# The conditioning by row, moved from a setup of its own to beside the first attention blocks

## The chip, the cores and the metric

One core of a Trainium2 chip. The metric is device time of one launch in microseconds (us); shorter is better. The median of three runs of the kernel before is 1063.24 us (1062.80 to 1065.88). The profiled execution took 1059.56 us.

## The reference

Two transformer layers on x of 8 batches x 512 rows x 128 channels, float32. Each layer has an attention and a feed-forward part, each modulated by six vectors per batch, which come from a condition c (8 x 128):

```python
mod = silu(c) @ wmod                      # 8 x 768: six vectors of 128 channels for each batch
sa, ca, ga, sb, cb, gb = split(mod, 6)    # names of the kernel: shift, scale and gate, twice
x = x + gate(ga) * attention(layernorm(x) * (1 + ca) + sa)
x = x + gate(gb) * ffn(layernorm(x) * (1 + cb) + sb)
```

Layer 0 is a plain one-headed softmax attention over 512 rows, then a gated feed-forward part whose operands are quantised in blocks of 16 (FP4 grid). Layer 1 is an attention of 16 heads with a decayed bias by position, then a feed-forward part with ternary weights.

## The kernel before, in words

Five engines each run one list of instructions, written out by Python generators that are stepped in a fixed interleaving; semaphores tie the lists together. `Chip.gate` (L70 on) is a barrier of all five engines, followed by the clearing of semaphores and by a second barrier.

**Setup** (`prepare`, from L149). SP's queue issues the loads in order: the conditions and `wmod` (L181, L182), seven side loads (L184 to L187), the eight batches of X (L189), the weights of both attentions (L1097, L1099). ACT makes Sigmoid and Ln of the decay logits (L1388 to L1392), Silu of the condition (L199), copies of the modulation (`mod`, L203), the powers of the decay (L1403 to L1405). PE multiplies by `wmod` in two forms: with batches as rows (L230), and with channels as rows (`by_channel`, L237). DVE makes decay tables (L1439 to L1451) and from `mod` the gates by row; from L267 on it adds the projected value bias, then splits the table `full` into three bfloat16 `parts` (L274 to L281). PE spreads each batch's row over all 128 partitions by a matmul with a 0/1 matrix, in two halves per batch (L245), and ACT (L208) and DVE (L285, L286) copy the halves to `rows`. DVE then copies the `chan` values (L289). POOL makes masks and constants up to L1425. A gate closes the setup.

**Layer 0** (`layer0`, from L888) runs attention and feed-forward as two threads. `attention0` has 48 blocks u, batch g = u / 4 and quarter a = u mod 4; 32 of them have attention work. In a block: DVE's row maximum of the scores (L481), ACT's Exp (L520), PE's transposes (L441), the next block's scores (L434), ACT's copy (L527). Beside these run the projections of the next batch: DVE's statistics (L356 to L367), POOL's power and shift (L375, L377), ACT's normalised rows (L387), PE's transposes (L339), ACT's modulated `hT` with `chan` (L391), and q, k, v (PE L343, L346, L350; ACT L396, L401, L406). Batch 0's projection stands ahead of block 0. DVE's `complete_dve` (L1455 to L1459) is in block 2. The residual uses `ga0` of `rows` (DVE L495, in u = 6 for batch 0), and POOL adds the bias row `bg0` (L561).

In each block a function `go` is called for four or five slots (five if u is even). Slot f, counted over all blocks, steps the feed-forward thread, whose parts start at constants: the weights' quantisation at `WEIGHTS` = 5 (DVE in `quantise_dve`, L576 to L602, nine steps for each of three weights, 11 slots apart; POOL L611; PE L801; ACT L809), the rows' norm at 33, the first hidden part at 40, the halves at 60. The feed-forward thread uses PSUM banks 0 to 3, the attention banks 4 to 7. Slots from 159 on also begin layer 1's operands. A gate closes layer 0 (L947 on), and it clears 27 semaphores.

**Layer 1** is the rest of the program: attention, then feed-forward.

Of the kernel before, what the change touches and what calls it, by code (L numbers as in the profile page):

```python
# [148 lines left out]
def prepare(c, t, sh, ahead):  # L149


    pe, dve, act, pool, sp, bank = c.pe, c.dve, c.act, c.pool, c.sp, c.bank
    own = ExitStack()
    with own:
        s_x, s_cond, s_side = c.signals("0", "x cond side", own)
        s_clear, s_fill, s_pick, s_made, s_silu, s_mod, s_rows, s_bvo, s_chan = c.signals("0", "clear fill pick made silu mod rows bvo chan", own)
        s_copied, s_step, s_parts = c.signals("0", "copied step parts", own)
        s_spread, s_kept_act, s_kept_dve = c.signals("0", "spread kept_act kept_dve", own)
# [16 lines left out]
        part = lambda n: full[:, order.index(n) * D:(order.index(n) + 1) * D]  # L175
        gates_ = [("ga0", mod[0][:, 0:D]), ("ga1", mod[1][:, 0:D]), ("gb0", mod[0][:, 3 * D:4 * D]), ("gb1", mod[1][:, 3 * D:4 * D])]
        by_channel = ((0, "sa0", 0, 0.0), (0, "ca0", 1, 1.0), (1, "sa1", 0, 0.0), (1, "ca1", 1, 1.0), (1, "sb1", 3, 0.0), (1, "cb1", 4, 1.0))

        def on_sp():
            for l in range(2):  # L180
                sp.dma_start(cT[l], t[f"cT{l}"]).then_inc(s_cond, 16)  # L181
                sp.dma_start(wmod[l], t[f"wmod{l}"]).then_inc(s_cond, 16)  # L182
            for l in range(2):
                sp.dma_start(bout[l], t[f"bout{l}"].partition_broadcast(W3)).then_inc(s_side, 16)  # L184
                sp.dma_start(bv[l], t[f"bv{l}"]).then_inc(s_side, 16)
                sp.dma_start(wo[l], t[f"wo{l}"]).then_inc(s_side, 16)
            sp.dma_start(w3s, t["w3s"].partition_broadcast(W3)).then_inc(s_side, 16)  # L187
            for b in range(B):
                sp.dma_start(tiles(sh.x(b)), t["x"][b].rearrange("(t p) c -> p t c", p=P)).then_inc(s_x, 16)  # L189
# [20 lines left out]
        def on_pool():  # L210
            for l in range(2):
                g = pool.memset(cs[l], 0.0)
            g.then_inc(s_clear, 1)
            for x, value in ((pick, 0.0), (sh.ident, 0.0), (sh.identh, 0.0), (sh.maskh, 0.0), (sh.neghalf, -0.5)):
                g = pool.memset(x, value)
            g.then_inc(s_fill, 1)
            pool.wait_ge(s_fill, 1)
            for k in range(G3):
                pool.affine_select(out=pick, in_=pick, compare_op=ALU.not_equal, fill=1.0, base=-32 * k, pattern=[[-1, B]], channel_multiplier=1).then_inc(s_pick, 1)
                pool.wait_ge(s_pick, k + 1)  # L220
            for i in (sh.ident, sh.identh):
                pool.affine_select(out=i, in_=i, compare_op=ALU.not_equal, fill=1.0, base=0, pattern=[[-1, P]], channel_multiplier=1)
            pool.affine_select(out=sh.maskh, in_=sh.maskh, compare_op=ALU.is_ge, fill=-1e30, base=0, pattern=[[-1, P]], channel_multiplier=1).then_inc(s_made, 1)
            pool.wait_ge(s_made, 1)
            ahead.constants_pool()

        def on_pe():
            pe.wait_ge(s_silu, 1)
            for l in range(2):
                m = pe.matmul(bank[1 + l][0:W3, :], cs[l], wmod[l][:, 2 * D:6 * D], start=True, stop=True)  # L230
            m.then_inc(s_mod, 1)
            pe.wait_ge(s_side, 7 * 16)
            for l in range(2):
                m = pe.matmul(bank[3][0:W3, l * D:(l + 1) * D], bv[l].to_broadcast([P, W3]), wo[l], start=True, stop=True)
            m.then_inc(s_bvo, 1)
            for i, (l, n, j, one) in enumerate(by_channel):
                m = pe.matmul(bank[0][:, i * B:(i + 1) * B], wmod[l][:, j * D:(j + 1) * D], cs[l][:, 0:B], start=True, stop=True)  # L237
            m.then_inc(s_chan, 1)
            pe.wait_ge(s_parts, 1)
            pe.wait_ge(s_pick, G3)  # L240
            for b in range(B):
                for half in range(2):
                    if b >= 2:
                        pe.wait_ge((s_kept_act, s_kept_dve)[half], b - 1)
                    pe.matmul(bank[4 + (2 * b + half) % 4], pick[:, b:b + 1].to_broadcast([W3, P]), parts[:, half * 512:(half + 1) * 512], start=True, stop=True).then_inc(s_spread, 1)  # L245

        def on_dve():
            ahead.tables_dve()
            dve.wait_ge(s_copied, 1)
            for k, (n, g) in enumerate(gates_):  # L250
                dve.tensor_scalar(tmp[k], g, 0.0, 0.5, ALU.is_ge, ALU.subtract)
                v = dve.scalar_tensor_tensor(tmp[4 + k], g, -1.0, g, ALU.mult, ALU.max)
            v.then_inc(s_step, 1)
            dve.tensor_copy(part("sb0"), mod[0][:, D:2 * D])
            dve.tensor_scalar(part("cb0"), mod[0][:, 2 * D:3 * D], 1.0, None, ALU.add)
            dve.wait_ge(s_step, 1)
            for k in range(4):
                v = dve.scalar_tensor_tensor(tmp[4 + k], tmp[4 + k], 0.25, tmp[k], ALU.max, ALU.mult)
            v.then_inc(s_step, 1)
            dve.wait_ge(s_step, 2)  # L260
            for k, (n, g) in enumerate(gates_):
                v = dve.tensor_scalar(part(n), tmp[4 + k], 2.0, None, ALU.mult)
            v.then_inc(s_step, 1)
            dve.wait_ge(s_bvo, 1)
            dve.wait_ge(s_side, 7 * 16)
            for l in range(2):
                v = dve.tensor_tensor(bvo[l], bank[3][0:W3, l * D:(l + 1) * D], bout[l], ALU.add)  # L267
            v.then_inc(s_step, 1)
            dve.wait_ge(s_step, 4)
            for l in range(2):  # L270
                dve.tensor_tensor(part(f"bg{l}"), part(f"ga{l}"), bvo[l], ALU.mult)
            dve.tensor_tensor(part("gb1"), part("gb1"), w3s, ALU.mult).then_inc(s_step, 1)
            dve.wait_ge(s_step, 5)
            dve.tensor_copy(parts, full).then_inc(s_step, 1)  # L274
            dve.wait_ge(s_step, 6)
            dve.tensor_tensor(left, full, parts, ALU.subtract).then_inc(s_step, 1)
            dve.wait_ge(s_step, 7)
            dve.tensor_copy(mid, left).then_inc(s_step, 1)
            dve.wait_ge(s_step, 8)
            dve.tensor_copy(parts[32:64, :], mid[32:64, :])  # L280
            dve.tensor_tensor(parts[64:W3, :], left[64:W3, :], mid[64:W3, :], ALU.subtract).then_inc(s_parts, 1)  # L281
            for b in range(B):
                dve.wait_ge(s_spread, 2 * b + 2)
                k = bank[4 + (2 * b + 1) % 4]
                dve.tensor_copy(sh.rows[1][:, b * D:(b + 1) * D], k[:, 0:D])  # L285
                dve.tensor_copy(sh.rows[2][:, b * 3 * D:(b + 1) * 3 * D], k[:, D:4 * D]).then_inc(s_kept_dve, 1)  # L286
            dve.wait_ge(s_chan, 1)
            for i, (l, n, j, one) in enumerate(by_channel):
                dve.tensor_scalar(sh.chan[n], bank[0][:, i * B:(i + 1) * B], one, None, ALU.add)  # L289

        on_sp()
        on_act()
        on_pool()
        on_pe()
# [1913 lines left out]
```

## Time and profile before

| | |
|---|---|
| median of three runs | 1063.24 us |
| profiled execution | 1059.56 us |
| its span, first to last instruction | 1058.3 us |
| busy PE, DVE, ACT, POOL | 869.2, 750.4, 659.3, 401.9 us |
| scores of block 0 end, gate of layer 0 | at 48.45 us, at about 342.7 us |

Times in the trace count from the first instruction. A row of the timeline has start, duration, engine, line, operation, and in brackets how long the engine was idle before it and what released it. A "q" behind an engine's name is its instruction queue (SPq issues DMAs). PEclk is the granted TensorE clock as a share of 2.4 GHz.

### The profile page before, as it was taken

Reading aid. Unit: us, or ns where it says so; the run is one execution under the profiler, and the core shown is the slowest. Engines: PE = TensorE matmul, PEld = TensorE weight load, DVE = VectorE, ACT = ScalarE, POOL = GpSimd, SP = SyncE. Lnnn points to the kernel's source line nnn. Section 1 sums busy time; section 2 is a strip of 40 time slices with the busy share of each in tenths; the row PEclk is TensorE's granted clock in tenths of the full one; section 3 lists DMA queues with packets and bytes.
Section 4 is the critical chain, followed back from the end, with each engine's and each line's share of the span. In section 5 each row is a group of like instructions: output and inputs, shape, how many; then the busy total and the mean of one; then the engine's idle time right before and its main releaser. Section 6 shows DMA issues by size and latency. Waiting matters only on the chain.

```text
span 1058.3 us, 25490 instructions
## 1 busy us (share of the span) xinstructions
PE 869.2 (82%) x9999; PEld 526.8 (50%) x9999; DVE 750.4 (71%) x1784; ACT 659.3 (62%) x1154; POOL 401.9 (38%) x664
## 2 busy tenths in 40 slices
PE   3577888877556689898989989899988868898987
PEld 1244455544335356565656656566655543444434
DVE  7366788888755778778687776868878647666653
ACT  4366878874522376756657566566666747776865
POOL 3024444444666547355354635437232210101000
PEclk7599999998967599999999999999999989999999
DMA  5000000000116235342523436154353000000000
GB/s 146 9 13 0 1 1 1 1 1 1 51 52 175 55 86 142 87 129 65 146 71 97 121 76 166 43 133 105 97 149 94 3 2 1 20 2 20 1 22 20
DMA packets 70698, 63.60 MB, mean 60 GB/s; under 512 B 30600, under 2 KB 62824, under 8 KB 70576
## 3 DMA queue, kind: packets, MB, share of 16 engines
q1 hardware_dynamic: 70064, 61.90, 22.1%
q8 instruction: 83, 1.36, 0.6%
q14 instruction: 39, 0.32, 0.1%
q10 hardware_dynamic: 512, 0.02, 0.0%
HBM read 34.02 MB, written 27.36 MB: 58 GB/s over the span
## 4 chain that ended last, share of the span: by engine, by line
PE 44%; DVE 11%; issue 6%; ACT 5%; POOL 2%; DVEq 0%; POOLq 0%; ACTq 0%
PE bank L2008 12%; PE bank L1589 7%; PE bank L1564 3%; PE bank L1537 3%; PE bank L1529 3%; PE bank L1545 3%; PE bank L1526 2%; PE bank L1519 2%; DVE bank L1672 1%; ACT 4g L2066 1%; PE bank L1555 1%; DVE 4f L2102 1%; PE bank L1597 1%; PE bank L1552 1%; DVE roots L1238 1%
## 5 line engine op out<-in xcount | busy, mean ns | idle before, releaser
L1750 ACT ACTIVATE ET<-bank 64x512 f32<-64x512 f32 x128 | 75.5, 590 | 101.4 <-PE bank L1555 100.5
L2089 DVE TENSOR_TENSOR act<-4f,act 128x512 f16<-128x512 f32 x96 | 66.4, 692 | 57.3 <-ACT act L2056 57.1
L1745 ACT ACTIVATE ET<-bank 128x768 f32<-128x768 f32 x128 | 103.2, 806 | 2.4
L1672 DVE TENSOR_TENSOR bank<-bank,W 128x256 f32<-128x256 f32 x128 | 54.7, 427 | 50.9 <-PE bank L1519 50.9
L1677 DVE TENSOR_TENSOR bank<-bank,WT 128x256 f32<-128x256 f32 x128 | 55.2, 431 | 49.9 <-PE bank L1545 49.9
L1682 DVE TENSOR_REDUCE mo<-bank 128x4 f32<-128x512 f32 x128 | 87.8, 686 | 2.7 <-PE bank L1529 2.5
L1589 PE MATMUL bank<-ET,vv 128*32 128x128 f32 (+2 forms) x1792 | 89.1, 323 | 0.8 <-DVE O L1707 0.8
L2056 ACT ACTIVATE act<-4f 128x512 f16<-128x512 f32 x96 | 60.4, 630 | 28.3 <-DVE 4f L2102 26.2
L1690 DVE TENSOR_REDUCE mo<-bank 128x3 f32<-128x384 f32 x128 | 70.0, 547 | 0.0
L1691 DVE TENSOR_REDUCE mo<-bank 128x3 f32<-128x384 f32 x128 | 69.9, 546 | 0.0
L1529 PE MATMUL bank<-maskq,identh 128*64 128x512 bf16 x256 | 62.7, 396 | 0.0
L2008 PE MATMUL bank<-act,std 128*128 128x512 f16 x256 | 58.1, 389 | 0.0
L2008 PE MATMUL bank<-act,cp 128*128 128x512 f16 x256 | 56.6, 379 | 0.0
L1526 PE MATMUL bank<-ring 128*64 128x128 f16 x256 | 28.1, 236 | 34.4 <-DVE bank L1672 34.4
L1589 PEld LDWEIGHTS bank<-ET,vv 128*32 128x32 f32 x1792 | 43.6, 109 | 23.8 <-issue 22.2
L1751 ACT ACTIVATE ET<-bank 64x256 f32<-64x256 f32 x128 | 48.6, 379 | 1.5
L2077 ACT ACTIVATE 4f<-bank,roots 128x512 f32<-128x512 f32 x64 | 43.3, 676 | 7.0 <-PE bank L2008 6.9
L1555 PE MATMUL bank<-maskk,identh 128*64 128x256 bf16 x256 | 47.3, 274 | 0.0
L1343 POOL TENSOR_TENSOR M<-cp 128x192 f32<-128x192 f32 (+2 forms) x48 | 23.4, 487 | 56.0 <-ACT cp L1294 54.9
L2126 POOL TENSOR_TENSOR X<-X,4Y 128x512 f32<-128x512 f32 x8 | 10.1, 1265 | 90.0 <-DVE 4Y L2115 90.0
L139 POOL TENSOR_TENSOR rstd<-ve,neghalf 128x4 f32<-128x4 f32 x8 | 9.3, 1164 | 91.9 <-DVE ve L121 91.9
L2008 PEld LDWEIGHTS bank<-act,std 128*128 128x128 f16 x256 | 25.7, 101 | 31.3 <-issue 3.6
(377 smaller groups left out, 2539.5 us busy)
## 6 DMA issues: line engine op xcount, KB each, us to landing
ring<-scr_q SPq DMA_DIRECT2D x16, 324.0 KB
QO<-scr_q SPq DMA_DIRECT2D x16, 324.0 KB
ring<-scr_a SPq DMA_DIRECT2D x16, 252.0 KB
KA<-scr_a SPq DMA_DIRECT2D x16, 252.0 KB
ring<-scr_k SPq DMA_DIRECT2D x16, 168.0 KB
KB<-scr_k SPq DMA_DIRECT2D x16, 168.0 KB
scr_a<-dk SPq DMA_DIRECT2D x8, 288.0 KB, 2.6
X<-in_x SPq DMA_DIRECT2D x8, 256.0 KB, 5.1
```

Of the source, the lines that this page charges most:

```text
L1529: m = pe.matmul(tiles(psD[z, :]), sh.identh[:, z], over(maskq, NT), start=False, stop=True, skip_group_check=True)
L1555: m = pe.matmul(half(psDT[z, :], 0), sh.identh[:, z], over(maskk, NT), start=False, stop=True, skip_group_check=True)
L1589: m = pe.matmul(psO[r:r + 32, c0:c1], vv[b % NV][:, v0:v0 + 32], ET[n % NE][:, e0:e0 + c1 - c0], start=c0 == 0, stop=k == NT - 1, skip_gro ...
L1672: dve.tensor_tensor(half(psD, 1), half(psD, 1), over(W[:, h * HB:(h + 1) * HB], NT), ALU.mult).then_inc(s_wq, 1)
L1682: dve.tensor_reduce(tiles(mo[g % 2][:, x * NT * NT:(x + 1) * NT * NT])[:, :, NT - 1], tiles(psD), AX.X, ALU.max).then_inc(s_ra, 1)
L1690: dve.tensor_reduce(to[:, 12:15], tiles(psX[:, 0:3 * P], 3), AX.X, ALU.max).then_inc(s_rb, 1)
L1691: dve.tensor_reduce(to[:, 6:11:2], tiles(psX[:, 512:512 + 3 * P], 3), AX.X, ALU.max).then_inc(s_rc, 1)
L1745: act.activation(ET[n % NE][:, T:SEG * P], psXT[:, 0:NP * P], ACT.Exp).then_inc(s_expo, 1)
L1750: act.activation(to[0:HB, :], psDT[0:HB, :], ACT.Exp)
L2008: m = pe.matmul(to, l, r, start=n == 0, stop=n == len(todo) - 1)
L2056: act.activation(act_[s][layer % 2][0][:, o * T:(o + 1) * T], f32_[f % 3], ACT.Copy).then_inc(s_hi, 1)
L2089: dve.tensor_tensor(lo, f32_[f % 3], hi, ALU.subtract).then_inc(s_lo, 1)
```

## The change

`prepare` has no barrier and no clearing of its own any more. It is called by `ffn0`, which passes it the first attention's thread. Its work is cut in two. The first part, ahead of block 0, keeps the loads, Silu, both products with `wmod` (`by_channel` first now), the gates by row and the decay tables, and takes in batch 0's statistics, normalised rows and `hT`. The second part (`rest`) is stepped once per slot f from slot 0 on: the value bias product, the making of `parts`, the spreading of the eight batches and the copies to `rows`. Waits that the barrier used to cover are written out.

```diff
 def on_sp():
     for l in range(2):  # cT and wmod, as before
+    sp.dma_start(tiles(sh.x(0)), ...).then_inc(s_x, 16)
+    ahead.load_first_sp()                 # wqkv0, wo0, bqk0
     ... seven side loads
-    for b in range(B): x -> s_x
-    ahead.load_sp()
-    sp.wait_ge(s_x, 16 * B)
+    for b in range(1, B): x -> s_rest
+    ahead.load_sp()
 def on_act():
-    ahead.decay_act()
+    ahead.load_act()
     ... wait s_cond, s_clear; Silu into cs
+    ahead.decay_act()                     # Sigmoid alone
+    first.begin_act(5)                    # batch 0's normalised rows
+    act.wait_ge(s_chans, 1)
+    first.begin_act(3)                    # batch 0's hT
     ... wait s_mod; copies to mod
-    ahead.powers_act()
-    for b in range(B): ... rows[0]
+    ahead.log_act()                       # Ln
 def on_pe():
     pe.wait_ge(s_silu, 1)
+    ... by_channel matmuls, s_chan
     ... mod matmuls, s_mod
-    ... bias matmuls; by_channel; spread
+    pe.wait_ge(s_made, 1)
 def on_dve():
+    dve.wait_ge(s_x, 16)
+    first.begin_dve()                     # batch 0's statistics
+    ahead.clamp_dve()
+    dve.wait_ge(s_chan, 1)
+    ... chan copies, s_chans
+    first.scale_dve()
     ahead.tables_dve()
     ... gates by row, as before
-    ... bias rows, parts, copies to rows, chan
+    ahead.exponents_dve()
+def rest_pe():
+    pe.wait_ge(s_side, 7 * 16)
+    ... bias matmuls, s_bvo
+    yield from blank(PARTS + 2)           # PARTS = 3
+    pe.wait_ge(s_parts, 1)
+    pe.wait_ge(s_pick, G3)
+    for b in range(B):
+        for half in range(2):
+            if b >= 2:
+                pe.wait_ge((s_rows, s_kept_dve)[half], b - 1)
+            pe.matmul(bank[(2 * b + half) % 4], ...).then_inc(s_spread, 1)
+        yield
+def rest_dve():
+    yield
+    ... bvo, bg, gb1
+    yield
+    ... parts, left
+    yield
+    ... mid, parts
+    yield from blank(PARTS)
+    for b in range(B):
+        dve.wait_ge(s_spread, 2 * b + 2)
+        ... two copies to rows[1], rows[2]
+        yield
+def rest_act():
+    yield from ahead.powers_act()         # three steps
+    yield from blank(PARTS)
+    for b in range(B):
+        act.wait_ge(s_spread, 2 * b + 1)
+        ... copy to rows[0]
+        yield
 # project_dve(b)
+        if b == 1:
+            dve.wait_ge(s_rest, 16 * (B - 1))
 # residual(g) on DVE
+            else:
+                dve.wait_ge(s_rows, B)
 # on_pool of attention0: bias row bg0
-            if a == 1 and g < B:
-                pool.wait_ge(s_xh, g + 1)
-                ... x(g) += bg0(g)
+            if a == 0 and 1 <= g <= B:
+                pool.wait_ge(s_xh, g)
+                if g == 1:
+                    pool.wait_ge(s_rows, B)
+                ... x(g - 1) += bg0(g - 1)
 # ffn0
-    WEIGHTS, ROWS, HIDDEN, MAIN, CYCLE = 5, 33, 40, 60, 18
+    WEIGHTS, ROWS, HIDDEN, MAIN, CYCLE = 17, 33, 40, 60, 18
 # layer0
     def go():
+        step(rest)
         step(thread)
         slot(next(f))
-    c.clear(first.signals)
+    c.clear(first.signals + [4 more] + rest.signals)   # 46 semaphores
 # complete_dve
+        dve.wait_ge(s_pow, 1)
```

Buffers of the setup (`full`, `parts` and so on) share their place with later feed-forward buffers, and the weights' own buffers no longer share it.

## Rows read from the trace of the kernel before

**Rows 1.** The page's first line.

```profile
span 1058.3 us, 25490 instructions
```

**Rows 2.** Windows: start:end, length, busy by engine (count), granted clock, DMA.

```profile
0.00:48.45 48.45, 20.66 (x54) 8.65 (x54) 25.03 (x81) 19.50 (x36) 9.29 (x36) 0.70 0.30 80
48.45:63.25 14.80, 9.79 (x27) 4.40 (x26) 10.56 (x31) 7.71 (x16) 2.43 (x3) 0.73 0.13 37
63.25:92.05 28.80, 21.71 (x94) 12.27 (x95) 16.28 (x62) 17.67 (x39) 12.40 (x14) 1.00 0.00 1
```

**Rows 3.** Timeline of SP's queue, and the DMA view's row of X.

```profile
2.70 0.43 SPq L184 DMA_DIRECT2D bout<-in_bout  x1
...
6.01 6.05 SPq L189 DMA_DIRECT2D X<-in_x  x8
...
X<-in_x SPq DMA_DIRECT2D x8, 256.0 KB, 5.1
```

**Rows 4.** Timeline of the setup, 5 to 23 us.

```profile
5.47 1.28 ACT L1391 ACT_TABLE_LOAD   x1
...
7.57 1.89 POOL L1425 MEMSET vv<- 128x608 f32 x3
...
8.39 0.70 ACT L199 ACTIVATE cs<-cT 128x8 f32<-128x8 f32 x6
...
9.14 3.40 PE L230 MATMUL bank<-wmod,cs 128*96 128x512 f32 x4 [9.14 <-ACT cs L199]
...
12.58 1.08 ACT L203 ACTIVATE mod<-bank 96x512 f32<-96x512 f32 x2 [3.49 <-PE bank L230]
...
12.81 1.40 PE L237 MATMUL bank<-cs,wmod 128*128 128x8 f32 x12
...
17.51 0.48 DVE L267 TENSOR_TENSOR bvo<-bank,bout 96x128 f32<-96x128 f32 x2
...
23.16 6.57 PE L245 MATMUL bank<-parts,pick 96*128 96x512 bf16 x16 [8.94 <-DVE parts L281]
```

**Rows 5.** Groups of instructions, 9 to 31 us: count, busy us, mean ns.

```profile
L286 DVE COPY rows<-bank 128x384 f32<-128x384 f32 x8 | 4.4, 547 | 0.0
...
L285 DVE COPY rows<-bank 128x128 f32<-128x128 f32 x8 | 2.3, 290 | 1.7 <-PE bank L245 1.1
```

**Rows 6.** Timeline of batch 0's projection, behind the gate.

```profile
32.09 0.86 DVE L356 BATCH_NORM_STATS2 stats<-X 128x6 f32<-128x128 f32 x4
...
34.90 0.20 POOL L377 TENSOR_TENSOR 1shift<-1nmean,rstd 128x4 f32<-128x4 f32 x1
35.22 1.65 ACT L387 ACTIVATE ring<-X,1shift,rstd 128x128 f32<-128x128 f32 x4 [5.07 <-POOL 1shift L377]
...
37.01 1.08 PE L339 MATMUL bank<-ident,ring 128*128 128x128 f32 x4 [7.28 <-ACT ring L387]
38.13 0.78 ACT L391 ACTIVATE ring<-bank,sa,ca 128x512 f32<-128x512 f32 x1 [1.27 <-PE bank L339]
...
41.82 2.08 PE L346 MATMUL bank<-ring,roots 128*128 128x512 f32 x2 [0.78 <-ACT ring L396]
...
48.49 0.69 DVE L481 TENSOR_REDUCE nm<-bank 128x1 f32<-128x512 f32 x1 [14.86 <-PE bank L434]
```

**Rows 7.** Timeline of blocks 1 to 3 and 8, DVE and PE.

```profile
52.91 0.69 DVE L481 TENSOR_REDUCE nm<-bank 128x1 f32<-128x512 f32 x1 [1.09 <-PE bank L434]
...
57.66 0.69 DVE L481 TENSOR_REDUCE nm<-bank 128x1 f32<-128x512 f32 x1 [0.95 <-PE bank L434]
...
59.64 0.56 DVE L599 TENSOR_TENSOR qb_u<-qb_u,qb_w 128x384 f32<-128x384 f32 x1
...
60.87 1.02 PE L346 MATMUL bank<-ring,roots 128*128 128x512 f32 x2
...
...
91.45 0.69 DVE L576 TENSOR_REDUCE qa_amax<-hm 128x32 f32<-128x512 f32 x1 [6.38 <-POOL hm L711]
```

**Rows 8.** One line's instructions (clearing of semaphores, L81): min/median/max ns.

```profile
L81 DVEq EVENT_SEMAPHORE_RANGE_CLEAR  x15: 54/54/56, 31.3 to 343.3; - x15
```

More of the change, by code:

```diff
@@ L146, in blank, with prepare @@
         yield
-def prepare(c, t, sh, ahead):
+class Thread:
+    pass
+def prepare(c, t, sh, ahead, first):
     pe, dve, act, pool, sp, bank = c.pe, c.dve, c.act, c.pool, c.sp, c.bank
+    s_cond, s_side = c.signals("0", "cond side", ahead.layer0)
+    s_clear, s_fill, s_pick, s_made, s_silu, s_mod, s_bvo, s_chan = c.signals("0", "clear fill pick made silu mod bvo chan", ahead.layer0)
+    s_copied, s_step, s_parts = c.signals("0", "copied step parts", ahead.layer0)
+    s_spread, s_kept_dve = c.signals("0", "spread kept_dve", ahead.layer0)
+    s_x, s_rest, s_chans, s_rows = first.s_x, first.s_rest, first.s_chans, first.s_rows
+    G3, W3 = 3, 96
+    order = [n for g in GROUPS for n in g]
     own = ExitStack()
     with own:
[L155 to L158, printed above, removed]
         sb = lambda *a, **k: c.sb(*a, at=own, **k)
-        G3, W3 = 3, 96
-        order = [n for g in GROUPS for n in g]
         cT = [sb(f"cT{l}", B) for l in range(2)]
@@ L174, in prepare @@
         pick = sb("pick", B, dt=BF16, rows=W3)
[L175 to L189, printed above, removed]
-            ahead.load_sp()
-            sp.wait_ge(s_x, 16 * B)
@@ L210, in on_pool @@
[L210 to L294, printed above, removed]
-        on_dve()
-        c.gate()
-        c.clear([s_x, s_cond, s_side, s_clear, s_fill, s_pick, s_made, s_silu, s_mod, s_rows, s_bvo, s_chan, s_copied, s_step, s_parts, s_spread, s_kept_act, s_kept_dve])
-        c.gate()
-class Thread:
-    pass
+    part = lambda n: full[:, order.index(n) * D:(order.index(n) + 1) * D]
+    gates_ = [("ga0", mod[0][:, 0:D]), ("ga1", mod[1][:, 0:D]), ("gb0", mod[0][:, 3 * D:4 * D]), ("gb1", mod[1][:, 3 * D:4 * D])]
@@ new lines, in prepare, with on_sp @@
+    by_channel = ((0, "sa0", 0, 0.0), (0, "ca0", 1, 1.0), (1, "sa1", 0, 0.0), (1, "ca1", 1, 1.0), (1, "sb1", 3, 0.0), (1, "cb1", 4, 1.0))
+    PARTS = 3
+    spread = lambda b, half: bank[(2 * b + half) % 4]
+    def on_sp():
+        for l in range(2):
+            sp.dma_start(cT[l], t[f"cT{l}"]).then_inc(s_cond, 16)
+            sp.dma_start(wmod[l], t[f"wmod{l}"]).then_inc(s_cond, 16)
+        sp.dma_start(tiles(sh.x(0)), t["x"][0].rearrange("(t p) c -> p t c", p=P)).then_inc(s_x, 16)
+        ahead.load_first_sp()
+        for l in range(2):
+            sp.dma_start(bout[l], t[f"bout{l}"].partition_broadcast(W3)).then_inc(s_side, 16)
+            sp.dma_start(bv[l], t[f"bv{l}"]).then_inc(s_side, 16)
+            sp.dma_start(wo[l], t[f"wo{l}"]).then_inc(s_side, 16)
+        sp.dma_start(w3s, t["w3s"].partition_broadcast(W3)).then_inc(s_side, 16)
+        for b in range(1, B):
+            sp.dma_start(tiles(sh.x(b)), t["x"][b].rearrange("(t p) c -> p t c", p=P)).then_inc(s_rest, 16)
+        ahead.load_sp()
@@ new lines, in on_act @@
+    def on_act():
+        ahead.load_act()
+        act.wait_ge(s_cond, 64)
+        act.wait_ge(s_clear, 1)
+        for l in range(2):
+            for g in range(G3):
+                a = act.activation(cs[l][:, 32 * g:32 * g + B], cT[l], ACT.Silu)
+        a.then_inc(s_silu, 1)
+        ahead.decay_act()
+        first.begin_act(5)
+        act.wait_ge(s_chans, 1)
+        first.begin_act(3)
+        act.wait_ge(s_mod, 1)
+        for l in range(2):
+            a = act.activation(mod[l], bank[1 + l][0:W3, :], ACT.Copy)
+        a.then_inc(s_copied, 1)
+        ahead.log_act()
@@ new lines, in on_pe, with on_dve @@
+    def on_pe():
+        pe.wait_ge(s_silu, 1)
+        for i, (l, n, j, one) in enumerate(by_channel):
+            m = pe.matmul(bank[0][:, i * B:(i + 1) * B], wmod[l][:, j * D:(j + 1) * D], cs[l][:, 0:B], start=True, stop=True)
+        m.then_inc(s_chan, 1)
+        for l in range(2):
+            m = pe.matmul(bank[1 + l][0:W3, :], cs[l], wmod[l][:, 2 * D:6 * D], start=True, stop=True)
+        m.then_inc(s_mod, 1)
+        pe.wait_ge(s_made, 1)
+    def on_dve():
+        dve.wait_ge(s_x, 16)
+        first.begin_dve()
+        ahead.clamp_dve()
+        dve.wait_ge(s_chan, 1)
+        for i, (l, n, j, one) in enumerate(by_channel):
+            v = dve.tensor_scalar(sh.chan[n], bank[0][:, i * B:(i + 1) * B], one, None, ALU.add)
+        v.then_inc(s_chans, 1)
+        first.scale_dve()
+        ahead.tables_dve()
+        dve.wait_ge(s_copied, 1)
+        for k, (n, g) in enumerate(gates_):
+            dve.tensor_scalar(tmp[k], g, 0.0, 0.5, ALU.is_ge, ALU.subtract)
+            v = dve.scalar_tensor_tensor(tmp[4 + k], g, -1.0, g, ALU.mult, ALU.max)
+        v.then_inc(s_step, 1)
+        dve.tensor_copy(part("sb0"), mod[0][:, D:2 * D])
+        dve.tensor_scalar(part("cb0"), mod[0][:, 2 * D:3 * D], 1.0, None, ALU.add)
+        dve.wait_ge(s_step, 1)
+        for k in range(4):
+            v = dve.scalar_tensor_tensor(tmp[4 + k], tmp[4 + k], 0.25, tmp[k], ALU.max, ALU.mult)
+        v.then_inc(s_step, 1)
+        dve.wait_ge(s_step, 2)
+        for k, (n, g) in enumerate(gates_):
+            v = dve.tensor_scalar(part(n), tmp[4 + k], 2.0, None, ALU.mult)
+        v.then_inc(s_step, 1)
+        ahead.exponents_dve()
@@ new lines, in rest_pe @@
+    def rest_pe():
+        pe.wait_ge(s_side, 7 * 16)
+        for l in range(2):
+            m = pe.matmul(bank[3][0:W3, l * D:(l + 1) * D], bv[l].to_broadcast([P, W3]), wo[l], start=True, stop=True)
+        m.then_inc(s_bvo, 1)
+        yield from blank(PARTS + 2)
[5 more added lines that the diff above has]
+                    pe.wait_ge((s_rows, s_kept_dve)[half], b - 1)
+                pe.matmul(spread(b, half), pick[:, b:b + 1].to_broadcast([W3, P]), parts[:, half * 512:(half + 1) * 512], start=True, stop=True).then_inc(s_spread, 1)
+            yield
@@ new lines, in rest_act @@
+    def rest_act():
[3 more added lines that the diff above has]
+            act.wait_ge(s_spread, 2 * b + 1)
+            act.activation(sh.rows[0][:, b * 4 * D:(b + 1) * 4 * D], spread(b, 0), ACT.Copy).then_inc(s_rows, 1)
+            yield
+    on_sp()
+    on_act()
+    on_pool()
+    on_pe()
+    on_dve()
+    rest = Thread()
+    rest.pe, rest.dve, rest.act, rest.signals = rest_pe, rest_dve, rest_act, [s_cond, s_side, s_clear, s_fill, s_pick, s_made, s_silu, s_mod, s_bvo, s_chan, s_copied, s_step, s_parts, s_spread, s_kept_dve]
@@ L305, in attention0 @@
+    return rest
 def attention0(c, t, sh, ahead):
@@ L318, in attention0 @@
     s_pv, s_out, s_rsum, s_proj, s_Y, s_add, s_bias = signals[20:27]
+    s_x, s_rest, s_chans, s_rows = c.signals("1", "x rest chans rows", ahead.layer0)
     wqkv, wo, bq, s_w = ahead.first_weights
@@ L626, in ffn0 @@
     s_hstep, s_hq, s_turn, s_kept, s_proj, s_Y, s_add = c.signals("2", "hstep hq turn kept proj Y add")
+    s_rows = first.s_add
+    names = ("wg", "wu", "wd")
+    wT = {n: sb(f"{n}T", FP) for n in names}
+    wr = {n: sb(f"{n}r", FP) for n in names}
+    room = lambda name, cols: [sb(f"{name}_{n}", cols // 16) for n in ("amax", "scale", "inv")] + [sb(f"{name}_{n}", cols) for n in ("u", "w")]
+    tmps_b = [room(f"qb{i}", 2 * FF) for i in range(2)]
+    rest = prepare(c, t, sh, ahead, first)
     xh, xq, Y, xqT = sb("2xh", T), sb("xq", T), sb("2Y", T), sb("xqT", T)
@@ L883, in ffn0 @@
     second = Thread()
+    second.rest = rest
     second.sp, second.pe, second.dve, second.act, second.pool, second.s_add = on_sp, on_pe, on_dve, on_act, on_pool, s_add
@@ L892, in layer0 @@
     first = attention0(c, t, sh, ahead)
-    second = ffn0(c, t, sh, ahead, first.s_add)
+    second = ffn0(c, t, sh, ahead, first)
+    rest = second.rest
     FREE = 159
@@ L943, in layer0 @@
     second.sp()
-    first.pe(beside(second.pe(), slot_pe))
-    first.act(beside(second.act(), slot_act))
-    first.dve(beside(second.dve(), slot_dve))
+    first.pe(beside(second.pe(), slot_pe, rest.pe()))
+    first.act(beside(second.act(), slot_act, rest.act()))
+    first.dve(beside(second.dve(), slot_dve, rest.dve()))
     first.pool(beside(second.pool(), slot_pool))
     c.gate()
-    c.clear(first.signals)
+    c.clear(first.signals + [first.s_x, first.s_rest, first.s_chans, first.s_rows] + rest.signals)
     c.gate()
```

97 lines of the change are left out of this document (64 added, 33 removed).

## The prediction

> **What bounds the kernel now.** I read the page for the span [rows 1], then windows of my own cut at the first score block, then the timeline of what stands ahead of it. The span is 1058.3 us. The profiled execution took 1059.56, 3.7 under the median of 1063.24; I work out a difference from the trace and take it off the median. About 0.3% (3.2 us) is what a measurement of this kernel can tell from no change.
>
> The first 48.45 us are poorly filled: PE works 20.7 of them, DVE 25.0, ACT 19.5 [rows 2]. What the reader is to see in the timeline is one long serial chain. The conditioning by row is DVE work until the spreading matmuls start at 23.16 [rows 4], and these with their copies go on until about 31. Only behind the gate, at 32.09, do batch 0's statistics start, and the first maximum of scores at 48.49 [rows 6]. None of the projection's inputs needs the rows: it needs X(0), `wqkv` and `chan`. From there on blocks follow each other as chains maximum, Exp, transposes, scores, and everything later moves with them. So the question is when the maximum of block 0 comes, and how much of that start the first blocks give back.
>
> **Start of block 0 after the change.** X(0) takes the place in SP's queue that the first side load has, 2.70, and lands 5.1 later [rows 3]: 7.8. Statistics to the variance take 1.5 (they start at 32.09; POOL's shift starts at 34.90, behind a power of about 1.1) [rows 6], so 9.3. POOL is in its memsets until 9.46 [rows 4], so its power and shift run from 9.5 to 10.8, and ACT's normalised rows (1.65) from 10.9 to 12.6 [rows 6].
>
> PE: Silu ran at 8.39, behind a table load of 1.28 [rows 4]. Now that load is the first thing on ACT and hides behind the DMA. I take the second `wmod` (issued about 2.2, with X's 5.1 to land) at 7.3, Silu done at 8.1. `by_channel` (1.40) ends at 9.5, the products for `mod` (3.40) at 12.9 [rows 4]. Transposes (1.08) end at 14.1, and `hT` (0.78) at 14.9, since `chan` is ready by 11. The q product takes 2.08 as the k product does [rows 6], to 17.0. ACT meanwhile copies `mod` (1.08, to 16.0), loads Ln's table (1.28) and makes two short Ln (about 0.3): 17.6 [rows 4]. So Ln, not PE, releases q's copy, at a price of 0.6. The copy (0.7) ends at 18.3. From the k product to the maximum it took 48.49 − 41.82 = 6.7 [rows 6]: block 0 starts at **25.0**, 23.5 us earlier.
>
> Is DVE there in time? Of its 25.0 us busy [rows 2] the part from 17.51 to 23.16, 5.6 us [rows 4], and the row copies, 4.4 + 2.3 = 6.7 [rows 5], leave. 12.7 stay. From 7.8 on they would be over at 20.5; the wait for `mod` at 16.0, once the tables are made, adds about 3: 23.5, just ahead of 25.0. DVE is the next stream to be late.
>
> The queues: SP issues X(0) past seven side loads, and the side loads and X(1) to X(7) wait behind the first weights. Eight X issues took 6.05 [rows 3], so the last X is issued by about 14 and lands by 19; batch 1's statistics ask for it at about 27. Side loads land by 13 and are asked for at 25. These edits cost nothing as long as the loads land within these 8 us; if not, DVE's queue stands still in block 0 by as much as is missing. POOL's bias row moves three blocks later and is still three quarters ahead of the residual's addition: nothing, and its new wait for the rows holds back POOL only if these come after block 4.
>
> **What the first blocks give back.** Slots 0 to 13 are blocks 0 to 2. They took 14.8 us [rows 2].
> - Block 0 (slots 0 to 4): DVE gets the 5.6 us of bias rows and parts in slots 1 to 3. It had 1.09 idle before the next maximum [rows 7]. Plus **4.5**. ACT's powers and the Exp table load (1.28, and about 1 us for each power) lie beside this, though the first delays the first Exp by about 0.7; DVE is longer, so it is not added.
> - Block 1 (slots 5 to 8): PE spreads batches 0 to 2 ahead of its transposes, a pair taking 6.57 / 8 = 0.8 at the lower clock [rows 4], and starts only when `parts` is there, as DVE's maximum does: 2.5 for PE. DVE's three pairs of copies take 2.5, against an idle 0.95 [rows 7]. DVE's count gives 1.6, PE's 2.5. I take **2.4**, since the transposes stand behind the matmuls.
> - Block 2 (slots 9 to 13): five more pairs of copies, 4.2, plus about 0.8 of waiting for matmuls that themselves wait for banks, less about 2.4 of weight quantisation that moves away. Plus **2.6**. `complete_dve` stays.
> Together 9.5. The bounds: nothing beyond DVE's bare excess gives 6; all 12.3 us of DVE work plus 0.8 with no cover gives 13. I keep 9.5: DVE was busy for 10.56 of these 14.8 us already [rows 2], so the cover is thin.
>
> **WEIGHTS from 5 to 17.** The weights' first two turns fall where the second and third fell. The third now runs in slots 39 to 47, beside the first hidden part. Seven of its nine DVE steps fall into blocks 9 and 10. One of the longest takes 0.56 [rows 7], so seven are at most 3.9; several work on 24 columns only, and I take 2.9; the first falls into the 6.38 us that DVE waits before 91.45 [rows 7]. Block 9 has idle time for half of it; the rest, and POOL's and PE's share, delay the first hidden part: **1.5**, between 0 and 6.
>
> **The end.** The gate of layer 0 clears 46 semaphores instead of 27 in three engines: 6.3 more at 54 ns [rows 8], with gaps **0.5**. The gate that is gone is in the 23.5.
>
> Sum: 23.5 − 9.5 − 1.5 − 0.5 = 12.0 faster: 1063.2 − 12.0 = **1051.3 us**.
>
> On table loads there is a rule. In the trace Ln's load takes 1.28, and the Ln starts at its end [rows 4]. The Trainium skill (ScalarE: Activation LUTs, "What ACT_TABLE_LOAD costs") gives the load the same time but adds a drain of about 1.38 to each switch. Two loads (Ln, Exp) could stand in the new chain, so by that rule the time would be some 2 to 3 us longer, 1054; the timeline before shows no such drain.
>
> **Rivals.**
> - *TensorE's clock is up sooner.* Before, the clock falls to 1.2 GHz in the idle stretches and averages 0.70 of full speed up to 48.45 [rows 2]; the k product takes 2.08 there and 1.02 once 2.4 GHz is granted [rows 6, 7]. Now PE's work lies closer together. Four such products in the chain at 1 us each, and 1 in block 1: 5 more, 1046. Against it: the projection's chain still has PE waiting for ACT between products. 0.15. The Trainium skill (TensorE: Matmul & The Clock Gate, "What's actually happening") lets the clock follow how busy PE was, which is the direction of this rival.
> - *The third weight delays the feed-forward's whole start.* Its 2.9 us on DVE, 0.8 on POOL, and PE's and ACT's short pieces all end up in front of the first hidden part: 6 instead of 1.5, 1056; for it, lists in fixed order; against it, idle time of DVE before 91.45. 0.15.
> - *The overlap is an illusion*: the moved work costs in the blocks what it cost before (13) and the weights 6: 1059 to 1062, no change. 0.07.
> - *Slower*: PE's waits for `parts` and for banks keep the clock at 1.2 GHz through blocks 3 to 8. These took 28.8 us with 21.7 us of PE at a clock of 1.00 [rows 2]; at half the clock that alone is 43.4, plus 14.6. With 2 more in blocks 1 and 2: 1068. It decides if projections in block 3 still take 2.08. Against it: PE is dense from block 1 on. 0.07.
> - That the change doesn't remove the gate can't be.
>
> **How the numbers follow.** The forecast of 1051 (1048 to 1055) has 0.56. The range takes in the clock's rival and the weights': 1045.5 to 1058. Faster by over 0.3% are forecast, clock and weights: 0.86. Within 0.3%: 0.07. Slower: 0.07.
>
> **What would show it.** In the changed profile: batch 0's statistics at 8, not 32; the first maximum at 25 (23 to 27); blocks 0 to 2 lasting 24 us; DVE idle-free through block 0; maximum of block 9 about 14 earlier than 92.05; layer 0's gate at 331. A first maximum after 30, or blocks 0 to 2 over 30, would make the forecast wrong.

## The result, and the profile of the changed kernel

The changed kernel takes 1045.45 us (median of 4 runs, 1043.87 to 1047.83) against 1064.03 for the kernel before (1062.80 to 1065.88, 4 runs): a ratio of 0.9824, interval 0.9804 to 0.9843, or 18.6 us. Forecast were 12.0, and 1045.5 as the lower end of the range. A second measurement in more rounds (below) gave a ratio of 0.9840 (0.9816 to 0.9864), 17.0 us. The kernel becomes faster, as forecast, but by about half as much again.

The windows of the changed kernel, cut at the same events as those of before: the maxima of blocks 0, 3, 9 and 31, and layer 1's first DVE work. Columns as in [rows 2].

```profile
0.00:26.19 26.19, 14.12 (x36) 7.90 (x37) 11.40 (x56) 11.47 (x24) 9.09 (x36) 0.87 0.54 147
26.19:47.81 21.62, 13.82 (x53) 6.92 (x52) 18.01 (x47) 14.76 (x29) 1.75 (x2) 0.84 0.09 25
47.81:74.43 26.62, 22.49 (x83) 12.10 (x82) 17.49 (x64) 16.07 (x37) 11.28 (x13) 0.87 0.00 1
74.43:215.78 141.35, 118.75 (x555) 73.09 (x553) 118.29 (x306) 115.96 (x202) 64.74 (x58) 1.00 0.00 1
215.78:326.28 110.50, 68.02 (x299) 47.14 (x300) 76.34 (x157) 42.52 (x79) 70.42 (x79) 0.80 0.24 68
326.28:1042.60 716.32, 630.19 (x8986) 382.14 (x8984) 505.35 (x1159) 456.74 (x786) 248.99 (x478) 0.97 0.27 72
```

Beside the same stretches of before, that gives a ledger (us; plus is time gained):

| stretch | before | after | gained | forecast |
|---|---|---|---|---|
| up to the first maximum | 48.49 | 26.19 | +22.3 | +23.5 |
| blocks 0 to 2 | 14.76 | 21.62 | −6.9 | −9.5 |
| blocks 3 to 8 | 28.80 | 26.62 | +2.2 | 0 |
| blocks 9 to 30 | 142.61 | 141.35 | +1.3 | −1.5 |
| block 31 to the end of layer 0 | 108.96 | 110.50 | −1.5 | −0.5 |
| layer 1 | 714.68 | 716.32 | −1.6 | 0 |
| sum | 1058.3 | 1042.6 | +15.7 | +12.0 |

The profiled executions are 1059.56 and 1043.87; the first lies 4.5 under its median and the second 1.6, which is the rest to 18.6. Two rows of the ledger say less than they seem to. Of the 1.3 in blocks 9 to 30, 1.7 are block 17, whose length changes by itself between executions (last section); without it the stretch is 0.4 longer. And the last two stretches, cut at DVE's last clearing of layer 0's semaphores, are 108.6 to 112.1 and 714.9 to 717.0 us long in seven of the traces (before, changed, experiments 1, 6, 7, 9 and 11), so their losses of 1.5 and 1.6 are within what two traces differ by.

The timeline of the changed setup, against [rows 4] and [rows 6]:

```profile
7.57 0.70 ACT L210 ACTIVATE cs<-cT 128x8 f32<-128x8 f32 x6 [3.58 <-DMA wmod<-in_wmod]
...
8.33 2.73 PE L242 MATMUL bank<-cs,wmod 128*128 128x8 f32 x12 [8.33 <-ACT cs L210]
8.41 0.87 DVE L393 BATCH_NORM_STATS2 stats<-X 128x6 f32<-128x128 f32 x4 [8.41 <-DMA X<-in_x]
...
10.91 3.71 PE L245 MATMUL bank<-wmod,cs 128*96 128x512 f32 x4
...
11.40 1.65 ACT L424 ACTIVATE ring<-X,1shift,rstd 128x128 f32<-128x128 f32 x4 [1.51 <-POOL 1shift L414]
...
14.41 1.06 PE L374 MATMUL bank<-ident,ring 128*128 128x128 f32 x4
...
16.40 1.12 PE L378 MATMUL bank<-ring,roots 128*128 128x512 f32 x2 [0.93 <-ACT ring L428]
17.33 1.28 ACT L1456 ACT_TABLE_LOAD   x1
...
18.62 0.21 ACT L1456 ACTIVATE lg<-lg 128x16 f32<-128x16 f32 x1
...
18.83 0.67 ACT L433 ACTIVATE ring<-bank,bq 128x512 f32<-128x512 f32 x1
...
26.19 0.69 DVE L518 TENSOR_REDUCE nm<-bank 128x1 f32<-128x512 f32 x1 [1.12 <-PE bank L471]
```

The reader is to see the forecast's chain, link by link: X(0) at 8.4 (forecast 7.8), the transposes held up by PE's own products with `wmod` (L245), and q's copy at 18.83 released by Ln, not by PE's product, which was over at 17.5. The last row shows DVE idle for 1.12 before the first maximum: DVE was in time, as forecast (25.1 against 26.2). Ln starts as its table's load of 1.28 ends; no drain stands between. The Trainium skill (ScalarE: Activation LUTs, "What ACT_TABLE_LOAD costs") adds one of about 1.38; by these rows the sum was right to leave it out.

The first blocks, against [rows 7]:

```profile
34.78 0.69 DVE L518 TENSOR_REDUCE nm<-bank 128x1 f32<-128x512 f32 x1
34.81 3.06 PE L288 MATMUL bank<-parts,pick 96*128 96x512 bf16 x6 [5.08 <-DVE parts L312]
...
40.56 0.69 DVE L518 TENSOR_REDUCE nm<-bank 128x1 f32<-128x512 f32 x1 [1.90 <-PE bank L471]
...
47.81 0.68 DVE L518 TENSOR_REDUCE nm<-bank 128x1 f32<-128x512 f32 x1
...
51.77 0.69 DVE L518 TENSOR_REDUCE nm<-bank 128x1 f32<-128x512 f32 x1 [2.82 <-PE bank L471]
```

Blocks 0 and 2 end without DVE idle: there DVE is the bound. Block 1 (5.8 us) waits for PE, whose spreading matmuls start only when `parts` is there. In block 3 DVE is idle for 2.82 again.

### The profile page after: what moved, and what is told of

Read it like the earlier page. It is cut to its first block, busy times and chain, and to the rows that moved or that the text cites. A ratio compares the mean times of both kernels' runs of the same rounds, so it can differ in the third digit from the quotient of the medians.

```text
span 1042.6 us, 25479 instructions
## 1 busy us (share of the span) xinstructions
PE 867.4 (83%) x9999; PEld 529.3 (51%) x9999; DVE 746.9 (72%) x1784; ACT 657.5 (63%) x1154; POOL 406.3 (39%) x664
## 4 chain that ended last, share of the span: by engine, by line
PE 45%; DVE 11%; issue 6%; ACT 5%; POOL 2%; DVEq 0%; POOLq 0%; ACTq 0%
PE bank L2081 12%; PE bank L1662 7%; PE bank L1637 3%; PE bank L1610 3%; PE bank L1602 3%; PE bank L1618 3%; PE bank L1599 2%; PE bank L1592 2%; DVE bank L1745 1%; ACT 4g L2139 1%; PE bank L1628 1%; DVE 4f L2175 1%; PE bank L1670 1%; PE bank L1625 1%; DVE roots L1299 1%
```

## The experiments

Times are compared by the ratio to the kernel before on the same chip; "over the changed kernel" is the difference of ratios to 0.9824, times 1064. By the second measurement of the changed kernel (0.9840) each such difference is 1.7 us smaller. Line numbers in rows are those of the changed kernel, plus up to five where an edit adds lines.

**1. The weights' later start alone, in the kernel before.**

```diff
-    WEIGHTS, ROWS, HIDDEN, MAIN, CYCLE = 5, 33, 40, 60, 18
+    WEIGHTS, ROWS, HIDDEN, MAIN, CYCLE = 17, 33, 40, 60, 18
```

> The kernel before with WEIGHTS = 17 alone; all is computed. Theory A (now mine): the later weights help, since the third weight's DVE, POOL, PE and ACT pieces no longer stand in front of batch 0's first hidden part; the stretch from block 3's to block 9's maximum falls from 28.8 us to about 26.6, and the time is 2 to 3 us under the kernel before. Theory B (the prediction's step): 1.5 us slower. Theory C (the 2.2 us seen in that stretch come from something else, such as the clock): no difference, within 1 us.

Measured: 1059.39, ratio 0.9940 (0.9920 to 0.9961): **6.0 us faster** than 1065.41 (4.2 to 8.5 by the interval), about twice what theory A said; theories B and C fall. So about a third of the whole gain needs no new order of the setup. Windows of this run from block 0's maximum to block 3's, block 9's and block 31's:

```profile
48.46:61.04 12.58, 8.96 (x25) 4.32 (x26) 7.19 (x21) 7.03 (x15) 2.43 (x3) 0.69 0.16 44
61.04:87.81 26.77, 22.40 (x89) 12.18 (x88) 17.09 (x64) 16.60 (x38) 11.29 (x13) 0.94 0.00 1
87.81:228.91 141.10, 118.76 (x555) 73.11 (x553) 119.53 (x306) 116.10 (x203) 62.56 (x58) 1.00 0.00 1
```

Against 14.76, 28.80 and 142.61 these are 2.2, 2.0 and 1.5 less. The first is DVE's: block 2 no longer holds the first weight's steps beside `complete_dve`. Of the second, 1.6 lie in block 8 and 0.7 in block 5. In block 8, before, ACT copied the third weight (from 85.59, after waiting for its transposition) ahead of the normed rows that the first hidden part is waiting for; in this run the norm goes first:

```profile
85.59 0.49 ACT L809 ACTIVATE wdT<-bank 128x384 f32<-128x384 f32 x1 [1.17 <-PE bank L801]
85.97 1.64 ACT L690 ACTIVATE 2xh<-X,shift,2rstd 128x128 f32<-128x128 f32 x4
```

```profile
81.70 1.64 ACT L690 ACTIVATE 2xh<-X,shift,2rstd 128x128 f32<-128x128 f32 x4
83.24 0.47 ACT L809 ACTIVATE wuT<-bank 128x384 f32<-128x384 f32 x1
87.21 0.69 DVE L576 TENSOR_REDUCE qa_amax<-hm 128x32 f32<-128x512 f32 x1 [3.62 <-POOL hm L711]
```

(the first of the kernel before, the second of this run; the changed kernel has the order of the second). Shift was ready at 84.16 before and at 81.51 here: 1.8 us of waiting became 0.2. DVE's first work on the hidden part, which stands ahead of block 9's maximum, comes 5.5 us behind the start of the norm in both (91.45 in [rows 7], 87.21 here), so block 9 gets the 1.6.

It is a matter of one slot. ACT copies the weights in slots 15, 26 and 37 before and in 27, 38 and 49 with `WEIGHTS` = 17; the norm is in slot 37, and where both share a slot the weight's copy comes first in ACT's list. The second weight now stands where the third stood, one slot later. `WEIGHTS` = 6, which would show this slot's worth by itself, was not run.

The third difference, 1.5, is block 17 (7.2 us before, 5.6 here), which is no effect of the edit (last section). So up to block 31 the trace shows 4.2 for the weights' move, the lower end of what the times show.

**2. The weights earlier in the changed kernel** (`WEIGHTS` = 9).

> The changed kernel with WEIGHTS = 9 in place of 17; all is computed. Theory A: the third weight is back in slots 31 to 39, in front of the first hidden part: about 2 us slower than the changed kernel, and the stretch from block 3's to block 9's maximum over 28 us. Theory B: 1.5 us faster than the changed kernel. Theory C: no difference.

Measured: 1050.79, ratio 0.9873 (0.9841 to 0.9906), 5.2 over the changed kernel. The direction is theory A's, the place is not: the stretch from block 3 to block 9 is 28.5, 1.9 more, but another 4.6 are lost in block 9 (8.0 us, in the changed kernel 3.4), of which block 10 gives 1.5 back. PE stands there:

```profile
76.87 0.84 POOL L663 TENSOR_TENSOR wdr<-qb_u,qb_scale 128x384 f32<-128x384 f32 x1
77.76 0.50 PEld L857 LDWEIGHTS bank<-ident,wdr 128*128 128x128 f32 x3 [7.03 <-POOL wdr L663]
77.76 0.90 PE L857 MATMUL bank<-ident,wdr 128*128 128x128 f32 x3 [6.20 <-POOL wdr L663]
```

DVE had finished this weight at 72.1. POOL took it up at 76.87, since its list has the next batch's power and shift, the first hidden part's modulation and a bias row before it; PE, in order, waited 6.20 with the attention's scores behind.

**3. The barrier back** (behind batch 0's `hT`).

```diff
+    first.begin_pe()      # batch 0's transposes, as before
+    first.begin_pool()    # batch 0's power and shift, as before
+    c.gate()
     second.sp()
```

> The changed kernel with one barrier of the five engines put back behind its setup, that is behind batch 0's hT and ahead of its q product. Theory A: the barrier costs what its last engine is late, and that is DVE with the exponents until 25.1 us, while q's product starts at 16.4: the first maximum comes at about 35.5 instead of 26.2, 9 us slower than the changed kernel. Rival: the barrier costs only its own drains, under 1 us, and the order of the work alone brings the gain.

Measured: 1055.87, ratio 0.9915 (0.9889 to 0.9941), 9.7 over the changed kernel; the first maximum is at 34.81, 8.6 later. DVE's last exponents and PE's wait for the barrier:

```profile
23.83 1.21 DVE L1527 TENSOR_TENSOR WT<-sq,bs 128x1024 f32<-128x1024 f32 x1
25.13 2.08 PE L378 MATMUL bank<-ring,roots 128*128 128x512 f32 x2 [9.68 <-DVEq L74]
```

PE waits 9.68 where it waited 0.93 without the barrier, and goes on 0.1 after DVE has ended (25.04). The rival falls: this barrier costs what its last engine is late.

**4. The second part in one piece** between block 0's scores and its maximum.

```diff
         scores(0)
+        step(beside.rest, 99)             # and so on DVE and ACT
...
         def go():
-            step(rest)
             step(thread)
```

> The changed kernel with the whole second part (value bias product, parts, spreading, copies to rows) run in one piece between block 0's scores and its maximum, not slot by slot. Theory A: idle time in blocks 0 to 2 covers nearly half of the moved work. In one piece it costs about 13 us ahead of the first maximum (39 instead of 26.2), blocks 0 to 2 fall from 21.6 to about 14.8, and the time is about 6 us over the changed kernel. Rival (the overlap is an illusion): as fast as the changed kernel, within 1 us.

Measured: 1055.13, ratio 0.9883 (0.9850 to 0.9916), 6.3 over the changed kernel. The first maximum is at 39.91 (13.7 later), and blocks 0 to 2 take 12.95, not 21.62. So the same work costs 13.7 in one piece and 8.7 slot by slot; blocks cover 5.0 of it. The rival falls.

```profile
39.91:52.86 12.95, 9.16 (x25) 4.22 (x26) 7.26 (x23) 6.92 (x15) 1.21 (x2) 0.74 0.16 42
```

This row also corrects the ledger: without the rest blocks 0 to 2 are 12.95 long, not 14.76, because the weights' move had emptied block 2 (12.58 in experiment 1).

**5. The bias row where it was** (block 4g + 1, waiting for all rows in block 1).

```diff
-            if a == 0 and 1 <= g <= B:
-                pool.wait_ge(s_xh, g)
-                if g == 1:
+            if a == 1 and g < B:
+                pool.wait_ge(s_xh, g + 1)
+                if g == 0:
```

> The changed kernel with POOL's bias row back where it was (block 4g + 1, so that for batch 0 POOL waits for all eight rows in block 1); all is computed. Theory A: nothing, within 1.5 us, for POOL has only batch 1's power before that and batch 2's power in block 4, long after the rows are there at about 47. Rival: the later place is needed, and POOL's standing wait holds up shift or weights: 2 us or more over the changed kernel.

Measured: 1047.25, ratio 0.9834 (0.9809 to 0.9859), 1.1 over the changed kernel, with intervals that overlap: the times tell no difference. The trace shows one of about that size. Block 2 is 8.3 us long instead of 7.25 (7.2 to 7.3 in experiments 3, 7, 8, 9 and 10). POOL's bias row of batch 0 now falls beside DVE's completion of the decay tables, and one small DVE instruction, 0.28 us in the changed kernel, lasts until the bias row has ended:

```profile
45.62 2.02 POOL L598 TENSOR_TENSOR X<-X,rows 128x512 f32<-128x512 f32 x1 [13.40 <-ACT rows L325]
46.43 1.29 DVE L1528 TENSOR_SCALAR Dq<-Dq,bsc 96x128 f32<-96x128 f32 x1
```

So the later place is worth about 1 us in block 2, though not for the reason that the rival names.

**6. The decay tables completed in block 3.**

```diff
-            if u == 2:
+            if u == 3:
                 ahead.complete_dve()
```

> The changed kernel with DVE's completion of the decay tables (2.7 us) in block 3 instead of block 2; all is computed. Theory A: block 2 (7.25 us) is bounded by DVE and block 3 has 2.8 us of DVE idle, so block 2 falls by about 2.4, block 3 stays, and the time is 2.4 us under the changed kernel. Rival: PE's spreading matmuls and their waits for banks bound block 2: no difference.

Measured: 1041.95, ratio 0.9791 (0.9769 to 0.9812), 3.5 under the changed kernel; the interval overlaps that of the first measurement (0.9804 to 0.9843) a little and that of the second (0.9816 to 0.9864) not. In the trace the maxima of blocks 2, 3 and 4 are at 38.75, 44.29 and 48.13: block 2 falls from 7.25 to 5.54, only 1.7, since then the last copy waits for PE (below); block 3 takes 3.8, not longer than the 4.0 of the changed kernel. The other 1.8 by which block 3 is earlier stood already at the first maximum (24.43), which this edit does not touch. So theory A holds with 1.7 for its 2.4.

```profile
43.62 0.29 DVE L316 COPY rows<-bank 128x128 f32<-128x128 f32 x1 [0.98 <-PE bank L288]
```

**7. PE kept busy ahead of Silu's products.**

```diff
 def on_pe():
+    pe.wait_ge(s_fill, 1)
+    for i in range(22):
+        pe.matmul(bank[6][:, 0:P], sh.neghalf, sh.neghalf, start=True, stop=True)
     pe.wait_ge(s_silu, 1)
```

> The changed kernel with 22 matmuls of constants (results overwritten unused) on PE from 1.7 to about 7.7 us, ahead of Silu's products; all is computed. Theory A (the prediction's clock rival): although the clock column says 1.00 up to 16 us, the products with wmod ran at the pace of 1.2 GHz (0.85 us for half of a 512-column product). With PE busy before, they halve: 6.1 us become about 3.2, the transposes come at 13.1 instead of 14.4, hT ends at 14.3, the first maximum comes 2 to 3 us earlier, and so does the end. Rival: the pace there is not the clock's; no difference.

Measured: 1042.84, ratio 0.9800 (0.9779 to 0.9822), 2.6 under the changed kernel, though the intervals overlap. The first maximum is at 23.62; in the traces whose setup is that of the changed kernel (its own and those of experiments 2, 5, 6, 8, 9 and 10) it lies between 24.43 and 26.21. So the edit gives 0.8 to 2.6 there.

```profile
1.74 7.33 PE L242 MATMUL bank<-neghalf 128*128 128x128 f32 x44 [1.74 <-POOL neghalf L227]
8.90 1.41 PE L245 MATMUL bank<-cs,wmod 128*128 128x8 f32 x12
10.16 1.94 PE L248 MATMUL bank<-wmod,cs 128*96 128x512 f32 x4
13.30 0.63 PE L377 MATMUL bank<-ident,ring 128*128 128x128 f32 x4 [1.21 <-ACT ring L427]
```

The products with `wmod` take 1.41 and 1.94 instead of 2.73 and 3.71: about half. The k product, too, takes 2.08 at 1.2 GHz and 1.02 at 2.4 [rows 6, 7]; so the changed kernel ran them at 1.2 GHz.

**8. The weights later still** (`WEIGHTS` = 20).

> The changed kernel with WEIGHTS = 20 in place of 17; all is computed. In slots 33 to 40 batch 0's rows are normed by a chain through DVE, POOL, ACT and POOL again; in the run with WEIGHTS = 9 PE stood 6.2 us for the third weight, which POOL had behind that chain. Theory A: what counts is that no weight's piece falls into that chain. With 20 the second weight's POOL piece is in slot 40 and PE's too, so it stands behind the chain as the third did with 9, and PE stands still: 4 to 6 us over the changed kernel. Theory B (the later the better, as DVE's load is what counts): 1 us faster than the changed kernel.

Measured: 1057.97, ratio 0.9942 (0.9921 to 0.9963), 12.6 over the changed kernel, twice what theory A said. "The later the better" falls. PE waits for the second weight, which POOL has behind the modulation, and for the third, which DVE works off beside the quantisation of the first rows (POOL itself waits 0.50 for it):

```profile
76.90 0.90 PE L857 MATMUL bank<-ident,wur 128*128 128x128 f32 x3 [6.21 <-POOL wur L663]
...
90.91 0.55 PE L857 MATMUL bank<-ident,wdr 128*128 128x128 f32 x3 [3.78 <-POOL wdr L663]
```

**9 to 11, on one chip: the changed kernel again, `WEIGHTS` = 14, and edits 6 and 7 together.**

> The changed kernel itself once more, on the same chip as the next two and in more rounds. All theories expect the ratio of the first measurement, 0.982 within 0.002. If it comes near 0.987, then the forecast of 12 us faster was right and the first measurement was off.

> The changed kernel with WEIGHTS = 14 in place of 17; all is computed. The weights' POOL and PE pieces fall on slots 23, 34 and 45; batch 0's chain of norms takes slots 33 to 40. Theory A (a piece costs only if PE meets it while POOL still has that chain ahead of it, as in slot 40): no difference to the changed kernel within 1.5 us, though DVE's load comes earlier. Theory B (the later the better): 1 to 3 us slower.

> The changed kernel with both edits that gained alone: the decay tables completed in block 3, and PE kept busy ahead of Silu's products; all is computed. If they act at different places (block 2, and the chain ahead of block 0) they add: 2.4 + 2 us under the changed kernel, ratio 0.978 to 0.976. Rival: DVE, which already ends the exponents just ahead of the first maximum, eats the second one: as fast as with the tables' move alone, 0.979.

Measured: 1048.21, ratio 0.9840 (0.9816 to 0.9864); 1050.85, ratio 0.9876 (0.9852 to 0.9900); 1040.79, ratio 0.9787 (0.9756 to 0.9818).

The first confirms 17 to 19 us, not 12. With 14 the kernel is 3.8 slower than with 17 on the same chip (the intervals overlap by 1.3 us), more than the 1.5 of theory A. It is nearest to theory B's 1 to 3, but experiment 8 speaks against "the later the better". Its trace names a place that I had not looked at: block 5 takes 6.2 us against 4.0, since the first weight's piece on PE (slot 23) meets POOL behind batch 2's power and shift and the bias row:

```profile
54.36 1.26 POOL L598 TENSOR_TENSOR X<-X,rows 128x512 f32<-128x512 f32 x1
...
55.59 0.83 POOL L663 TENSOR_TENSOR wgr<-qb_u,qb_scale 128x384 f32<-128x384 f32 x1
...
56.47 0.55 PE L857 MATMUL bank<-ident,wgr 128*128 128x128 f32 x3 [2.64 <-POOL wgr L663]
```

So the wait is of the same kind as in experiments 2 and 8, PE for POOL, but slots 33 to 40 are not its only place. Block 7 (5.1 against 4.1) was not followed up. The two edits together are the fastest version here, 5.6 under the changed kernel on the same chip (the intervals just touch), yet hardly under edit 6 alone. In the traces block 3's maximum comes at 43.28 against 47.06, 3.8 earlier, and layer 0 ends 2.3 earlier: block 17, 7.2 us long in this trace and 5.5 in the other, takes 1.7 back (last section). DVE has no idle time left before the first maximum in experiments 6, 7 and 11; whether this is what keeps the second edit from adding its part stays open.

## Why the prediction was wrong

- **Start of block 0** (forecast 25.0, 23.5 earlier): right, 26.19 and 22.3. `by_channel` took 2.73, not 1.40, and PE released the transposes at 14.4 instead of 13.0; q's product took 1.12, not 2.08, but Ln hid that. A barrier at this place costs 8.6 of it (experiment 3).
- **What the blocks give back** (9.5, of 6 to 13): 6.9, too dear by 2.6, within its bounds. Block 0 cost 4.2 more (forecast 4.5), block 1 1.0 (2.4), block 2 1.7 (2.6). In block 1 PE's three pairs of spreads took 3.06 and not 2.5, at a clock of 0.50, but before, PE had waited there 2.05 for batch 1's normalised rows (ahead of L339 at 54.92), and the spreads fell into that wait; the forecast had counted no cover for PE. In block 2 PE ran at 2.4 GHz (clock 1.00 from 40 us on), and the pairs of spreads, priced at 0.8, took 0.6. Experiment 4 says that the order slot by slot saves 5.0 over one piece.
- **WEIGHTS from 5 to 17** ("1.5, between 0 and 6" slower): this is the step that failed, by its sign. Experiment 1 measured 6.0 faster (4.2 to 8.5), and its trace 4.2. The forecast had 2.4 of it inside block 2's sum, where the trace shows 2.3; outside of block 2 it had 1.5 slower, and the trace shows 1.9 faster. The prediction wrote that the first two turns "fall where the second and third fell". They fall one slot later, and this slot takes a weight's copy out from in front of the norm on ACT: 1.6 us in block 8. And the third weight beside the first hidden part, for which the 1.5 stood, costs nothing that shows: blocks 9 to 11 take 11.9 us in experiment 1 as before.
- **The sum.** Up to block 31 the changed trace is 17.2 us ahead without block 17's 1.7, and 12.5 were forecast. Of the 4.7 between them the start gives −1.2, blocks 0 to 2 give +2.6, blocks 3 to 8 +2.2 and blocks 9 to 30 +1.1. So the weights outside of block 2 are 3.3, and what the blocks give back is nearly as large. The forecast with the weights' net 0.9 replaced by the measured 6.0 gives 17.1, close to the second measurement's 17.0; that is partly luck, for it leaves out the other errors, which nearly cancel, and the 6.0 is known to 2 us only.
- **The clock's rival** (5 more, 1046, 0.15): the time came out at this rival's figure, but not by its mechanism. Of its four products in the chain q's alone was fast (1.12); k's at 19.55, v's at 22.41 (2.08 each) and the scores (1.88) were at the pace of 1.2 GHz, and q's gain was hidden by Ln. Experiment 7 found 0.8 to 2.6 us of it still to be had in the setup. k's product got 1.13 in experiment 6, with the same setup. The Trainium skill (TensorE: Matmul & The Clock Gate, "What's actually happening") has the clock follow how busy PE was, and these runs agree.
- **The queues, POOL's bias row** (nothing): DVE never waits for X(1). The bias row's later place is no loss; experiment 5's trace makes it a gain of about 1 us in block 2.
- **Slower** and **no change**: not seen. Blocks 3 to 8 ran at a clock of 0.87, lower than the 1.00 of before, but took 2.2 us less all the same.
- **Range**: its lower end, 1045.5, allowed for the clock alone; a gain by the weights' move was not thought of, so no case stood below.

## What to carry to other kernels

When lists in fixed order are interleaved by slot numbers, moving a side task by some slots is a change of its own: measure it alone, over several places (here 9, 14, 17 and 20 gave ratios 0.987, 0.988, 0.982 to 0.984 and 0.994). One slot can be enough to swap two pieces on one engine's list. Before placing a piece, look on every engine's list at what stands ahead of it, above all on the helper that an in-order PE waits for. A barrier costs the lateness of its last engine, and work put into blocks costs what their idle time doesn't cover, so empty the full block first.
